# Attention scores from full-height products, or from pairs of half-height products on two halves of the partitions

## The reference, cut to what matters

```python
q = rope((x @ wq.T).reshape(b, t, 8, 64));  k = rope((x @ wk.T).reshape(b, t, 8, 64))
scores = einsum('bhtd,bhsd->bhts', q, k) / SCALING        # 8 maps, inner width 64
probs = softmax(scores, axis=-1).reshape(b, 4, 2, t, t)
diff = probs[:, :, 0] - lam * probs[:, :, 1]              # 4 heads, two maps each
attn = einsum('bhts,bhsd->bhtd', diff, v)
```

## Time and profile before

| | |
|---|---|
| Time, median of 2 runs | 3913.32 us (3910.45 to 3916.2) |
| The profiled execution, span | 4009.9 us |
| TensorE busy | 3462.3 us, 86% |
| VectorE busy | 2606.1 us, 65% |
| ScalarE busy | 1993.6 us, 50% |
| GpSimd busy | 1442.9 us, 36% |
| Mean granted TensorE clock | 0.935 |

### The profile page before, as it was taken

How to read it: one execution, slowest core, us unless ns; L and a number is a source line. 1 busy time by engine, 2 the same in 40 slices (tenths; PEclk the granted TensorE clock), 3 DMA queues, 4 the chain that set the end, 5 groups by cost and what they waited for, 6 DMA issues and landing times. The chain is left out here.

```text
span 4009.9 us, 61177 instructions
## 1 busy us (share of the span) xinstructions
PE 3462.3 (86%) x18948; PEld 2965.3 (74%) x18948; DVE 2606.1 (65%) x4553; ACT 1993.6 (50%) x3642; POOL 1442.9 (36%) x1496
## 2 busy tenths in 40 slices
PE   8999969998989989898888985299999999999990
PEld 7888859777777777777777774178887788878870
DVE  6777759888878878888887884244444444444434
ACT  2222228766666666666666661144444344444434
POOL 0000000344343433343443435344454545554442
PEclk9999989999999999999999996599999999999995
DMA  6666675434443433443442421255555555555548
GB/s 241 226 229 225 220 219 115 105 91 104 103 102 88 116 89 87 115 98 78 114 101 78 116 67 48 96 161 153 150 166 166 151 152 156 162 168 144 151 126 342
DMA packets 287215, 563.59 MB, mean 141 GB/s; under 512 B 35744, under 2 KB 102880, under 8 KB 282352
## 3 DMA queue, kind: packets, MB, share of 16 engines
q1 hardware_dynamic: 248624, 493.24, 40.7%
q0 software_dynamic: 36032, 50.60, 7.1%
q10 hardware_dynamic: 2304, 16.78, 1.0%
HBM read 375.19 MB, written 185.54 MB: 140 GB/s over the span
## 5 line engine op out<-in xcount | busy, mean ns | idle before, releaser
L709 DVE TENSOR_REDUCE att_neg_max<-att_ps_s 128x1 f32<-128x1024 f32 x512 | 623.1, 1217 | 181.2 <-PE att_ps_s L497 138.8
L627 ACT ACTIVATE att_prob<-att_ps_s,att_neg_max 128x1024 f32<-128x1024 f32 x512 | 573.6, 1120 | 326.0 <-DVE att_neg_max L709 274.9
L525 PE MATMUL att_ps_o<-att_v,att_diff_hi 128*128 128x256 f32 x2048 | 523.2, 293 | 17.8 <-issue 9.2
L526 PE MATMUL att_ps_o<-att_v,att_diff_lo 128*128 128x256 f32 x2048 | 502.3, 283 | 0.0
L496 PE MATMUL att_ps_s<-att_k_hi,att_q 128*128 128x512 f32 x1024 | 432.6, 423 | 78.0 <-issue 46.0
L1040 POOL TENSOR_TENSOR exp_w_lo<-exp_w_raw,exp_w_hi 128x2816 fp32r<-128x2816 f32 x63 | 401.5, 6373 | 272.9 <-ACT exp_w_hi L1031 272.9
L820 POOL DMA_INDIRECT slots<-att_entry,att_slot x390 | 398.7, 1022 | 248.0 <-DVE att_token L767 131.7
L497 PE MATMUL att_ps_s<-att_k_lo,att_q 128*128 128x512 f32 x1024 | 427.1, 417 | 0.0
L525 PEld LDWEIGHTS att_ps_o<-att_v,att_diff_hi 128*128 128x128 f32 x2048 | 391.9, 191 | 23.9 <-issue 23.4
L526 PEld LDWEIGHTS att_ps_o<-att_v,att_diff_lo 128*128 128x128 f32 x2048 | 393.0, 192 | 0.0
L666 DVE SCALAR_TENSOR_TENSOR att_diff<-att_prob,att_weight 128x1024 f32<-128x1024 f32 x256 | 328.0, 1281 | 5.1
(11 more groups left out here) (216 smaller groups left out, 8735.3 us busy)
## 6 DMA issues: line engine op xcount, KB each, us to landing
exp_w_raw<-in_w_t SPq DMA_DIRECT2D x64, 1408.0 KB
att_q<-q_parts SPq DMA_DIRECT2D x132, 256.0 KB
att_k_hi<-k_parts SPq DMA_DIRECT2D x132, 256.0 KB
att_k_lo<-k_parts SPq DMA_DIRECT2D x132, 256.0 KB
att_v<-v_parts SPq DMA_DIRECT2D x33, 1024.0 KB
v_parts<-proj_v_out SPq DMA_DIRECT2D x64, 512.0 KB, 3.4
exp_w_raw<-in_w_t SPq DMA_DIRECT2D x64, 512.0 KB, 3.9
proj_x_raw<-in_x_t SPq DMA_DIRECT2D x17, 1024.0 KB, 7.1
```

The costliest lines, as they stand in the source:

```text
L525: nc.tensor.matmul(ps_o[:, 0 : 2 * VD], diff_hi[i][:, t, :], v_buf[h % 2][:, t, :], start=t == 0, stop=False)
L526: last = nc.tensor.matmul(ps_o[:, 0 : 2 * VD], diff_lo[i][:, t, :], v_buf[h % 2][:, t, :], start=False, stop=t == TILES - 1)
L627: nc.scalar.activation(prob[s][i][:], ps_s[s][:], ACT.Exp, bias=neg_max[:, s, i : i + 1], accum_out=total).then_inc(exp_done[s], 1)
L709: nc.vector.tensor_reduce(neg_max[:, s, i : i + 1], ps_s[s][:], AX.X, ALU.max, negate=True).then_inc(max_done[s], 1)
```

## The change

Each product has 64 rows. q and k of a head each get one buffer per slot, of the same layout: the partitions hold the two maps (64 each), and the second axis the high and the low part. For each half of the keys there are three combinations of the parts (high by high, high by low, low by high), and for each of them one product of map 0 on partitions 0 to 63 and one of map 1 on partitions 64 to 127. A turn has 12 products in place of 8, and both waits on `exp_done` come ahead of the first of them. The last two products raise `s_done[0]` and `s_done[1]`. The product of low by low is left out. A head's q and k come in 8 transfers of 256 KB in place of 12.

```diff
-    LOADS_QK = 12
+    LOADS_QK = 8
-        k_hi = [st.sbuf(f"k_hi{i}", [P, 2, SEQ], F32R) for i in range(2)]
-        k_lo = [st.sbuf(f"k_lo{i}", [P, 2, SEQ], F32R) for i in range(2)]
+        k_buf = [st.sbuf(f"k{i}", [P, 2, SEQ], F32R) for i in range(2)]
...
-            src = slice(2 * h * FREQ, (2 * h + 2) * FREQ)
-            for part in range(2):
+
+            for sub in range(2):
+                src = slice((2 * h + sub) * FREQ, (2 * h + sub + 1) * FREQ)
                 for ri in range(2):
-                    def rows(parts, p):
-                        return parts[b, p, ri, src, :].rearrange("(s f) t -> f s t", s=2)
-
-                    at = 2 * part * FREQ + ri * FREQ
-                    sp.dma_start(q_buf[i][at : at + FREQ].bitcast(F32), rows(q_parts, part)).then_inc(qk_in[i], DMA)
-                    sp.dma_start(k_hi[i][at : at + FREQ].bitcast(F32), rows(k_parts, 0)).then_inc(qk_in[i], DMA)
-                    sp.dma_start(k_lo[i][at : at + FREQ].bitcast(F32), rows(k_parts, 1)).then_inc(qk_in[i], DMA)
+                    at = sub * HALF + ri * FREQ
+                    sp.dma_start(q_buf[i][at : at + FREQ].bitcast(F32), q_parts[b, :, ri, src, :].rearrange("l f t -> f l t")).then_inc(qk_in[i], DMA)
+                    sp.dma_start(k_buf[i][at : at + FREQ].bitcast(F32), k_parts[b, :, ri, src, :].rearrange("l f t -> f l t")).then_inc(qk_in[i], DMA)
...
                     for s in range(2):
                         if not (first and jl == 0):
                             pe.wait_ge(exp_done[s], j)
-                        for half in range(2):
-                            cols = slice(half * CHUNK, half * CHUNK + CHUNK)
-                            nc.tensor.matmul(ps_s[s][:, cols], q_buf[h % 2][:, s, q_cols], k_hi[h % 2][:, s, cols], start=True, stop=False)
-                            last = nc.tensor.matmul(ps_s[s][:, cols], q_buf[h % 2][:, s, q_cols], k_lo[h % 2][:, s, cols], start=False, stop=True)
-                        last.then_inc(s_done[s], 1)
+                    for half in range(2):
+                        cols = slice(half * CHUNK, half * CHUNK + CHUNK)
+                        for n, (q_part, k_part) in enumerate(((0, 0), (0, 1), (1, 0))):
+                            for s in range(2):
+                                rows = slice(s * HALF, s * HALF + HALF)
+                                last = nc.tensor.matmul(ps_s[s][:, cols], q_buf[h % 2][rows, q_part, q_cols], k_buf[h % 2][rows, k_part, cols], start=n == 0, stop=n == 2)
+                                if half == 1 and n == 2:
+                                    last.then_inc(s_done[s], 1)
```

## The result

| | before | after |
|---|---|---|
| Median of the timed runs | 3913.32 us | 3984.88 us (3984.29 to 3985.47) |
| Ratio after / before, 95% interval | | 1.0185 (1.0155 to 1.0214) |
| The profiled execution, span | 4009.9 us | 3982.6 us |
| TensorE busy in it | 3462.3 us | 3394.5 us |
| Mean granted TensorE clock | 0.935 | 0.947 |

The change made the kernel 1.9% slower; 3.9% was forecast. The profiled execution of the changed kernel agrees with its timed runs, while that of before was 97 us longer than its own. So the two recorded spans stand the wrong way round, and a difference of the two traces explains nothing. The first experiment therefore records the kernel before once more.

A forecast was written before the change was run, and what follows sets the result against it. It took a chain through scatters, ScalarE and VectorE, with TensorE waiting, to bound the loop. 35 + 112 + 11 - 6 = +152 us on the 4009.9 us span gave 4162, or 4065 us (+3.9%) timed; range 3955 to 4250.

The forecast's parts named there:

- Part 1: On TensorE the two score products of a pair stream together: 12 products take 1.39 us, saving 0.46 us a turn.
- one by one: Rival: the pairs of score products on TensorE do not overlap and start 0.23 us apart; 4226 us, chance 0.20.
- Part 2: Both waits ahead of all 12 score products, maps ending together: +35 us in batch 0, +112 us in batches 1 to 7.
- Part 3: TensorE's changes between full and half height in each turn: 140 x 0.08 us, +11 us.
- the ring: Batch 0's circle from scores over maximum and exponentials back to TensorE, closed by the new wait: 6.15 us a turn, 4.91 before.
- the way through the scatters: In a loop period, turn 3's later maximum delays scatters, diff_hi and map 1's exponential: turn 1's maximum +0.56 us.
- the half clock in turn 1: TensorE, idle longer before turn 1's scores, may run 2 us of them at half clock: 1.0 us more a period.
- Part 4: 8 transfers in place of 12 let the first scores start earlier, -6 us; fewer later loads change nothing.
- The late release is the profiler's: Rival: turn 0's late diff_hi may explain the profiled execution's extra 97 us; without it +0.5 a period, 3970 us, chance 0.17.
- The wait is covered: Rival: map 1's read ends before TensorE reaches the next scores, so 118 us is gained; 3789 us, chance 0.06.

The follow-up runs named there:

- w_first: The kernel before with both exp_done waits moved ahead of its eight full-height products: 3985.12 us, ratio 1.0191.
- w_inter: The kernel before with both waits first and its full-height products alternating between the maps: 4069.16 us, ratio 1.0412.
- hi_first: The changed kernel with ScalarE's diff_hi moved ahead of map 0's exponential: 3942.47 us, ratio 1.0080 to the kernel before.
- b_again: The kernel before, recorded once more with no edit: 3911.68 us, span 3910.0 us.
- six_six: The changed kernel with map 0's wait and six products first, then map 1's wait and six: 3928.83 us, ratio 1.0049 to the kernel before.
- a_12loads: The changed kernel with four more 256 KB transfers a head into an unread buffer, 12 in all: 4038.03 us, ratio 1.0314 to the kernel before.
- b_8loads: The kernel before with 8 transfers a head, k's second copies left out after the first heads, so scores differ from the reference: 3849.61 us, ratio 0.9824.
- a_late: The changed kernel with the next head's q and k loaded in a head's fourth turn, not its second: 3946.65 us, ratio 1.0086 to the kernel before.

## Why the direction was right and the size wrong

**Part 1 held.** Pairs start within 0.04 us of each other and follow 0.23 to 0.24 apart (0.31 or 0.34 for the first step). Only the ends are dearer: twelve products and the step to the transposes take 1.59 us in place of 1.39, so TensorE saves 0.26 us a turn and not 0.46. The rival *one by one* fell. One reason given for the 1.39 was misread: a map has six products in place of four, but a partition, which carried the products of both maps, now carries six in place of eight.

**Part 2 held in batch 0, and in the loop in part by luck.** Batch 0's turn was forecast at 6.15 and is 6.27 us; the stage gained 42.5 where 35, with 2 of Part 3, were in the sum. w_first shows that the wait alone does most of it (+27), w_inter that the common end adds to it, hi_first that the ring through ScalarE is what closes. In the loop 1.5 to 2.5 us a period were forecast, 2.0 taken, and 1.73 measured, 97 us in place of 112 (with Part 3's share 121). This came out near for partly wrong reasons: the way through the scatters and the half clock in turn 1 were those of one execution. In b_again the period is 25.9 us. Turn 0 gains 1.06 (there the ring closes too, which I had hidden under the scatters), turn 2 gains 0.75 (forecast 0.98), turns 3 and 1 next to nothing (+0.03 and -0.11).

**Part 3 had the right size for another reason.** The maximum starts 1.66 after the first product in place of 1.58, the 0.08 that I took. But the first step behind a wait is 0.31 us in the changed kernel and in w_first alike, and w_first changes no shape. So on the ring the 0.08 is the wait's and not the shape's; that it fits is luck. The shape shows where TensorE does not wait. In six_six the step into half height, 1350.70 to 1351.03, is 0.33 where b_again has 0.24, the step behind the first product 0.34 where it has 0.23, and the step out, 1352.88 to 1353.21, 0.33 where it has 0.23: 0.2 us in and 0.1 out.

The Trainium skill (TensorEngine Tiling (Array Packing), Key Properties) says that a change of tiling mode drains TensorE. The longer steps of six_six agree with it in kind. Behind a wait this case shows no price for it on the way in.

**Part 4 is the step that failed.** It said: "Later loads are issued a head ahead, with the DMA engines 40% busy; SyncE's four issues less delay nobody." The start was right (-6.8, taken -6). But the loads delayed the landing of the scatters (GpSimd's wait ends 7.4 to 7.8 us after the last one beside 12 loads, 3.1 to 4.2 beside 8, 1.2 beside none), and through `att_entry` the statistics, `x1_buf` and TensorE, in three turns of each batch. Fewer loads gave back 53 us (a_12loads against after) to 66 (b_8loads against before). With 12 transfers on both sides the change is +3.1% by measurement (a_12loads), with 8 on both +3.5% (against b_8loads); +3.9% was forecast.

I judged the queue by its share of busy time, and never asked what shares it. The first record also kept most of it out of sight: its periods were 2.7 us longer at turns 0 and 1, its wait row had 9 entries of this kind where b_again has 30, and turns 10, 18 and 26 were 6.6 us in most batches, over 5.3 for most others, where b_again has 9.2 to 10.2 over 6.5. Yet the sign stood in it: GpSimd's wait on the scatters ended 7.6 to 7.8 us after the last one in these periods and 1.2 in the others, just as in b_again. The same cover works for the changed kernel: of b_again's 10.1 us a batch, 5.8 are left in a_12loads, under turns that are longer by themselves, and 0.5 with 8 transfers. That is -30 and -37 us over seven batches.

Set beside each other by their medians, the last two parts cancel: the common wait is +75 (w_first), half height with the pairs another +53 (a_12loads against w_first), the fewer transfers -53. The second is the other surprise: under a common wait the pairs are a loss against w_first, since both maps end together and map 0's maximum starts 1.66 after the first product in place of w_first's 1.20. By the other path, with 8 transfers throughout, it is -66 for the transfers (b_8loads), +79 for half height with the old waits (six_six) and +56 for the common wait with the pairs side by side. On both paths half height is a loss. After, TensorE saves 0.26 us a turn and map 0's maximum starts 0.5 us later; in six_six TensorE saves nothing (2.18 for 1.83) and the maximum starts 0.6 us later.

**The rivals.** *The late release is the profiler's* was right in its first half: b_again shows `diff_hi` 2.7 us earlier. It was wrong in what it made of that. Without the late release I had left a period +0.5, since I let only the way from turn 2 to turn 3 count; measured is +1.73, since the ring closes at turn 0. That its time (3970) is near the one measured comes from the transfers, which it did not have either. *The wait is covered* fell: the wait is met 190 times.

**What stays open.** The last turn of a batch costs 11.1 us in b_again, 14.5 after, 12.3 in b_8loads, 12.9 in six_six and 8.7 to 10.0 with loads or `diff_hi` elsewhere. It is 20 us of the result, and it moves with the place of the loads and with the order on ScalarE. What differs is the length of a pause of TensorE at the loop's branch, for which the profile shows no semaphore. Here it is after and in a_late:

```profile
1232.92 2.50 PE L495 MATMUL att_ps_s<-att_k,att_q 64*128 64x512 f32 x10 [8.45 <-issue]
```

```profile
1223.12 2.83 PE L495 MATMUL att_ps_s<-att_k,att_q 64*128 64x512 f32 x12 [3.25 <-issue]
```

After, the DMA engines are busy with the eight loads for most of this pause; in a_late they are nearly idle from 1.8 to 8.3 us into the turn (stretch by busy time, DMA share last but one):

```profile
1221.00:1230.50 9.50, 3.47 (x29) 3.15 (x28) 3.99 (x11) 4.45 (x11) 6.12 (x6) 0.89 0.99 209
```

```profile
1215.50:1222.00 6.50, 4.37 (x37) 4.05 (x35) 4.92 (x11) 4.46 (x11) 3.21 (x3) 1.00 0.03 5
```

The trace has a kind of DMA packet called `instruction`. The first of them in that turn starts 11.4 us into it after and 6.3 in a_late. This fits a transfer of code that stands behind the loads, as the scatters do, but no run tests it. The experts' stage has the same code in all kernels and takes 1333 to 1360 us; after it is 11 us shorter than in b_again. No run shows why. Why one execution of before released ScalarE late is open too.

## What to carry to other kernels

When the recorded execution stands well off the timed runs, record it again before costing steps on it: the chain that bounds the one may not exist in the others. Count for a removed transfer what else lands beside it, above all small indirect transfers that an engine waits for; an average share of the DMA engines says nothing on that. Look in the record at when such waits end, also where they cost nothing yet. Measure each half of a change at equal transfers. And if two products can overlap by themselves, don't tie their inputs to one wait for it, and let the one whose result is wanted first end first.

## What the runs showed of the hardware

- Products on different row halves overlap even where six of one half are issued ahead of the six of the other: 12 products of 512 columns take 2.25 us to the last result, with a later product starting 0.70 us before an earlier one.
- Where TensorE does not wait, entering half height costs two longer steps (0.33 for 0.24 and 0.34 for 0.23 us) and leaving it one (0.33 for 0.23), in six_six against b_again.
- The first step behind a wait is 0.31 us at full height (w_first) and at half height (after).
- 12 transfers of 256 KB issued beside six indirect scatters let the wait for their landing end 7.7 us after GpSimd was through with the last; beside 8 it is 3.1 to 4.2 us, beside none 1.2. Without the four extra transfers a head, VectorE's waits of this kind fall from 30 to 10 in the whole kernel.
- One execution of the same program, 97 us longer than the others, had ScalarE's copy in turn 0 start 6.23 us after the turn's first product, where another had 3.57, and about 1.1 us behind the last indirect scatter.
- At a loop's branch TensorE paused 8.5 us after the change, with the DMA engines 99% busy for most of it, and 3.3 us in a_late, with the same loads elsewhere. What it waits for is not shown.
